# The MLP's first products: one four-byte pass becomes three rounded passes, and the gates move into the products' place

## The reference, cut to what matters

```python
DIM = 128
DEPTH = 2
HID = int(DIM * 4 * 2 / 3)
...
    x = x + o @ wo
    h = shift_token(x)
    mu = h.mean(-1, keepdims=True)
    var = h.var(-1, keepdims=True)
    h = (h - mu) / jnp.sqrt(var + 1e-05) * lg + lb
    h = h @ w1 + b1
    a, g = jnp.split(h, 2, axis=-1)
    h = a * jax.nn.gelu(g, approximate=False)
    x = x + h @ w2 + b2
```

## Time and profile before

| | |
|---|---|
| device time, median of 3 runs | 1245.42 us (1241.07 to 1248.66) |
| profiled execution | 1247.89 us |
| its span in the profile | 1246.1 us |
| busy: PE, DVE, ACT, POOL | 998.1, 798.1, 703.9, 390.8 us |
| mean granted PE clock | 0.922 of full speed |

### The profile page before, as it was taken

One profiled execution on the slowest core, in us unless ns is written; L12 is line 12 of the kernel. 1 busy time (PEld: TensorE's weight loads), 2 busy tenths in 40 slices (PEclk: granted clock), 3 DMA queues, 4 the chain that ended last, 5 costly groups with the idle time before them and its releaser, 6 DMA issues.

```text
span 1246.1 us, 22091 instructions
## 1 busy us (share of the span) xinstructions
PE 998.1 (80%) x8250; PEld 602.5 (48%) x8272; DVE 798.1 (64%) x1381; ACT 703.9 (56%) x1500; POOL 390.8 (31%) x251
## 2 busy tenths in 40 slices
PE   4079986069985788889889898989898898898886
PEld 2023333013323666666556665656565665666652
DVE  4088825058825668678677685867677786676751
ACT  3037763017773567557566565656666576576662
POOL 5000015000003553534444434342434435344330
PEclk9589998569997799999899999999999999999998
DMA  2950001950002211011010010000001010101100
GB/s 65 129 100 9 1 1 38 113 70 2 1 2 51 57 23 22 19 22 23 18 24 14 18 23 18 14 18 14 18 14 23 19 23 19 23 14 35 31 10 17
DMA packets 38268, 36.01 MB, mean 29 GB/s; under 512 B 11478, under 2 KB 30224, under 8 KB 38160
## 3 DMA queue, kind: packets, MB, share of 16 engines
q1 hardware_dynamic: 34708, 31.46, 13.8%
q10 hardware_dynamic: 3456, 3.15, 1.2%
HBM read 15.41 MB, written 4.21 MB: 16 GB/s over the span
## 4 chain that ended last, share of the span: by engine, by line
PE 28%; DVE 13%; POOL 11%; ACT 9%; issue 6%; POOLq 0%; DVEq 0%; ACTq 0%
PE psum L1165 6%; PE psum L1138 5%; POOL f_A L976 4%; POOL f_A L971 4%; ACT f_PW L1272 4%; PE psum L1052 3%; PE psum L1078 2%; PE psum L1089 2%; DVE f_A L1391 2%; DVE f_BS L1395 2%; POOL f_HL L963 2%; DVE f_NM L1423 2%; DVE f_SS L1402 2%; PE psum L1100 2%; PE psum L1158 1%
## 5 line engine op out<-in xcount | busy, mean ns | idle before, releaser
L1272 ACT ACTIVATE f_PW<-psum,f_NM 128x128 f32<-128x128 f32 x512 | 139.3, 383 | 127.9 <-DVE f_NM L1423 127.9
L500 DVE TENSOR_REDUCE a_M<-psum 128x1 f32<-128x512 f32 x256 | 160.2, 684 | 67.5 <-remote 38.7
L976 POOL TENSOR_TENSOR f_A<-f_A,f_RN 128x1024 f32<-128x1024 f32 x64 | 121.7, 1902 | 252.3 <-ACT f_RN L1283 250.0
L971 POOL TENSOR_TENSOR f_A<-f_A,f_BS 128x1024 f32<-128x1024 f32 x64 | 151.6, 2368 | 46.5 <-DVE f_BS L1395 45.0
L430 PE MATMUL psum<-a_KS,a_QS 128*128 128x512 bf16 x238 | 96.7, 413 | 79.7 <-DMA a_KS<-minus_ones 75.9
L547 ACT ACTIVATE a_PT<-psum 128x1024 f32<-128x1024 f32 x128 | 126.4, 1018 | 56.5 <-PE psum L452 56.1
L1391 DVE TENSOR_TENSOR f_A<-psum,cos 128x512 f32<-128x512 f32 x128 | 87.9, 686 | 93.5 <-ACT f_SQ L1240 93.5
L1052 PE MATMUL psum<-const,f_A 128*128 128x128 f32 x512 | 76.8, 299 | 49.6 <-POOL f_A L976 49.6
L452 PE MATMUL psum<-a_QS,a_KS 128*128 128x512 bf16 x252 | 94.5, 390 | 14.6 <-DMA a_QS<-a_MROW 10.4
L1423 DVE TENSOR_REDUCE f_NM<-psum 128x4 f32<-128x512 f32 x128 | 82.3, 685 | 36.4 <-PE psum L1078 36.4
L1042 PE MATMUL psum<-f_wqkv_h,f_HH 128*128 128x512 f32 x192 | 86.7, 451 | 23.0 <-DVE Y L1460 13.1
(11 more groups left out here) (173 smaller groups left out, 1966.5 us busy)
## 6 DMA issues: line engine op xcount, KB each, us to landing
f_VS<-f_V SPq DMA_DIRECT2D x112, 130.0 KB, 2.3
parts<-a_PRT ACTq DMA_DIRECT2D x24, 128.0 KB, 2.4
a_QS<-parts SPq DMA_DIRECT2D x8, 256.0 KB
a_KS<-parts SPq DMA_DIRECT2D x8, 256.0 KB
a_QS<-parts SPq DMA_DIRECT2D x4, 384.0 KB
a_KS<-parts SPq DMA_DIRECT2D x4, 384.0 KB
raw<-L_ffn_wqkv_dram SPq DMA_DIRECT2D x2, 768.0 KB, 7.0
a_XT<-L_attn_a_x_dram SPq DMA_DIRECT2D x4, 256.0 KB, 4.0
```

The costliest lines, as they stand in the source:

```text
L500: nc.vector.tensor_reduce(M[:, u % 4, k // 4, k % 4:k % 4 + 1], psum[:, bank("tile", i), :], AX_X, ALU.max)\
L971: nc.gpsimd.tensor_tensor(A[:, k % 2, :, :], A[:, k % 2, :, :], BS[:, k % 2, :, :], ALU.add)\
L976: nc.gpsimd.tensor_tensor(x, x, RN[:, k % 2, :, None].to_broadcast([P, 2 * HW, DW]), ALU.mult)\
L1272: last = nc.scalar.activation(PW[:, u % 4, c, :], psum[:, bank("scores", u), P * c:P * c + P], ACT.Exp, bias=NM[:, u % 4, c:c + 1])
```

## The change

The weights `w1` get a high part `w1_h` and a low part `w1_l`, for both layers at once (1364 columns). They are made at the start of `stream`: ACT waits for all weights and copies `w1_h` before it begins the plan, and POOL subtracts `w1_l` after its first three clears. For each group DVE rounds `mid` into `MH`, right after the bias, and POOL finds `ML = mid - MH` in the norm step. PE makes 18 products in `F32R` in place of the six plain ones, and waits for `mid_low` in place of `ln_done`. The buffer `gates` is gone: ACT writes the gates into `hidden`, once `w2` of the group before has read it, and DVE multiplies there in place. The raw `w1` lies in `hidden` until it is split, and `OUT` lies in `QB` and `NEG`.

```diff
-        w1 = sb("w1", [P, LAYERS, 2 * HID])
+        w1_h = sb("w1_h", [P, LAYERS, 2 * HID], F32R)
+        w1_l = sb("w1_l", [P, LAYERS, 2 * HID], F32R)
...
+        MH = sb("MH", [P, T], F32R)
+        ML = sb("ML", [P, T], F32R)
...
-        gates = sb("gates", [P, 3, T])
         hidden = sb("hidden", [P, 3, T])
+        w1 = hidden[:, :, :].rearrange("p b t -> p (b t)")[:, 0:LAYERS * 2 * HID]\
+            .rearrange("p (l n) -> p l n", l=LAYERS)
...
                 nc.gpsimd.memset(V[:, :, :, DW:DW + 1], 1.0).then_inc(s("zeroed"), 1)
+                pool.wait_ge(s("w1_high"), 1)
+                nc.gpsimd.tensor_tensor(w1_l[:, :, :], w1[:, :, :], w1_h[:, :, :].bitcast(F32), ALU.subtract)\
+                    .then_inc(s("w1_low"), 1)
                 nc.gpsimd.memset(VB[:, :, P:P + HA], 1.0).then_inc(s("ones_b"), 1)
...
                         pool.wait_ge(s("y_mid"), i + 1)
                         if i:
-                            pool.wait_ge(s("up"), 3 * i)
+                            pool.wait_ge(s("mid_low"), i)
...
+                    elif stage == "var" and norms[i][0] == "mlp":
+                        j = norms[i][1]
+                        pool.wait_ge(s("mid_high"), j + 1)
+                        if j:
+                            pool.wait_ge(s("up"), 3 * j)
+                        nc.gpsimd.tensor_tensor(ML[:, :], mid[:, :], MH[:, :].bitcast(F32), ALU.subtract)\
+                            .then_inc(s("mid_low"), 1)
...
-                        pe.wait_ge(s("ln_done"), i + 1)
+                        pe.wait_ge(s("mid_low"), i + 1)
                         for blk, (lo, w) in enumerate(HID_BLOCKS):
                             for kind, first in (("gate", HID), ("up", 0)):
-                                nc.tensor.matmul(take(kind, 3 * i + blk)[0:w, :],
-                                                 w1[:, layer, first + lo:first + lo + w],
-                                                 mid[:, :], start=True, stop=True).then_inc(s(kind), 1)
+                                dst = take(kind, 3 * i + blk)[0:w, :]
+                                of = slice(first + lo, first + lo + w)
+                                nc.tensor.matmul(dst, w1_h[:, layer, of], MH[:, :], start=True, stop=False)
+                                nc.tensor.matmul(dst, w1_l[:, layer, of], MH[:, :], start=False, stop=False)
+                                nc.tensor.matmul(dst, w1_h[:, layer, of], ML[:, :], start=False, stop=True)\
+                                  .then_inc(s(kind), 1)
...
                     nc.scalar.activation(wqkv_h[:, 0, cols], g.raw[:, cols], ACT.Copy).then_inc(s("weights_high"), 1)
+                act.wait_ge(s("weights"), 16 * len(weights))
+                nc.scalar.activation(w1_h[:, :, :], w1[:, :, :], ACT.Copy).then_inc(s("w1_high"), 1)
                 for stage, i in plan:
...
                             if i:
-                                act.wait_ge(s("hidden"), 3 * i + blk - 2)
-                            nc.scalar.activation(gates[0:w, blk, :], psum[0:w, bank("gate", 3 * i + blk), :],
+                                act.wait_ge(s("w2"), i)
+                            else:
+                                act.wait_ge(s("w1_low"), 1)
+                            nc.scalar.activation(hidden[0:w, blk, :], psum[0:w, bank("gate", 3 * i + blk), :],
                                                  ACT.Gelu, bias=b1[0:w, layer, 3 + blk:4 + blk])\
...
                             nc.vector.tensor_scalar(mid[:, :], mid[:, :], vecs[:, layer, 1:2], None, ALU.add)\
                               .then_inc(s("ln_done"), 1)
+                            dve.wait_ge(s("ln_done"), j + 1)
+                            if j:
+                                dve.wait_ge(s("up"), 3 * j)
+                            nc.vector.tensor_copy(MH[:, :], mid[:, :]).then_inc(s("mid_high"), 1)
```

More of the change, by code:

```diff
@@ L886, in stream @@
         OF = sb("OF", [P, T])
-        OUT = sb("OUT", [P, 2, 4, P])
+        OUT = [x[:, :].rearrange("p (t d) -> p t d", t=4) for x in (QB, NEG)]
         def pieces():
@@ L936, in _ @@
                         dst = out[k:k + 1].rearrange("a (t p) d -> p (a t) d", p=P)
-                        sp.dma_start(dst, OUT[:, k % 2, :, :]).then_inc(s(f"stored{k % 2}"), 16)
+                        sp.dma_start(dst, OUT[k % 2]).then_inc(s(f"stored{k % 2}"), 16)
                 for slot in range(4):
@@ L1360, in _ @@
                             act.wait_ge(s(f"stored{i % 2}"), 16 * (i // 2))
-                        nc.scalar.activation(OUT[:, i % 2, :, :].rearrange("p t d -> p (t d)"),
+                        nc.scalar.activation((QB, NEG)[i % 2][:, :],
                                              psum[:, bank("store", i), :], ACT.Copy).then_inc(s("out_copied"), 1)
@@ L1465, in _ @@
                             dve.wait_ge(s("gated"), 3 * i + blk + 1)
-                            if i:
-                                dve.wait_ge(s("w2"), i)
                             nc.vector.scalar_tensor_tensor(
                                 out=hidden[0:w, blk, :], in0=psum[0:w, bank("up", 3 * i + blk), :],
-                                scalar=b1[0:w, layer, blk:blk + 1], in1=gates[0:w, blk, :],
+                                scalar=b1[0:w, layer, blk:blk + 1], in1=hidden[0:w, blk, :],
                                 op0=ALU.add, op1=ALU.mult).then_inc(s("hidden"), 1)
```

## The result

The changed kernel takes 1257.61 us (median of 6 runs, 1254.85 to 1263.17) beside 1246.95 us of the kernel before (median of 6, 1235.48 to 1249.16). The ratio measured is 1.011, with a 95% interval of 1.0062 to 1.0159 (the two medians alone give 1.0085, inside it): slower, by about 1% and clear of the noise. The profiled execution took 1255.01 us, its span is 1253.2 us.

A forecast was written before the change was run, and what follows sets the result against it. It took DVE's maxima and ACT's line to bound each w1 step, PE adding 0.25 us in ten of 16 groups. Start +9.8, groups +2.1 and +1.8, last two -0.7 and -0.3 gave +12.7 us: 1258 us (1250 to 1266).

The forecast's parts named there:

- Start of `stream`: Head of the last part: ACT's copy waits for the last weight DMA, POOL's subtraction follows; first rotation sum +9.8 us.
- The second rival: The start costs little because later idle stretches take up most of the delay: about 1250 us, chance 9%.
- The cast: Norm step: DVE's rounding of mid between bias and maxima delays the maxima and ACT's line by 0.46 us a group.
- L1406 would be short: Norm step: this DVE maximum falls from 1.31 to 0.17 us without POOL's sum beside it, but gains nothing.
- The gates: w1 step: ACT's three gates shorten from 2.08 to 1.83 us in ten groups, -0.25 us each, since products end sooner.
- PE's gain of 1.0 us a group: w1 step: 18 rounded products take 4.3 us instead of 5.32; PE's busy time falls by some 15 us.
- ML and what it pushes: Norm and w1 steps: POOL's 1.28 us subtraction delays rotation sum and scaling, with 1.3 us to spare, costing nothing.
- the moved sum: Norm step: POOL's rotation sum could block DVE's cast or bias if already begun, but now stands behind both.
- The last groups: Groups 14 and 15, partly at half clock: faster products give -0.7 us and, after cast and subtraction, -0.3 us.
- The first rival: PE is the bound after all: fourteen groups gain 1.0 us each, the last two about 3 together; 1238 us, 5%.
- The third rival: PE, idle 1 us longer in each w1 step, falls to half clock more often: 1270 us, chance 7%.

The follow-up runs named there:

- run 1: Changed kernel with the two w1 transfers issued first and ACT waiting for these alone: 1249.19 us, ratio 1.0044 to the kernel before.
- run 2: As run 1, with the cast of mid into MH moved from DVE to POOL: 1243.2 us, ratio 0.9983 to the kernel before.
- run 3: Changed kernel with six plain four-byte products of the high parts, low-part products left out: 1261.3 us, ratio 1.0135 to the kernel before.
- run 4: Changed kernel with six rounded products of the high parts, low-part products left out: 1255.4 us, ratio 1.0088 to the kernel before.
- run 5: As run 2, with six plain four-byte products of the high parts, low parts left out: 1246.51 us, ratio 1.0008 to the kernel before.
- run 8: As run 7, plus cast, subtraction and PE's wait for them, but the old plain products of mid: 1256.43 us, ratio 1.0073 to the kernel before.
- run 6: As run 2, with DVE's bias after the maxima and POOL's cast and subtraction between rotation sum and scaling: 1238.81 us, ratio 0.9953 to the kernel before.
- run 7: Kernel before with only the gates' place changed, written into hidden and multiplied there in place: 1246.51 us, ratio 1.0013 to the kernel before.
- run 9: As run 6, with six plain four-byte products of the high parts, low parts left out: 1253.78 us, ratio 1.0039 to the kernel before.
- run 10: Kernel before with only the bias of mid moved behind the maxima on DVE: 1245.26 us, ratio 0.9998 to the kernel before.

## Why the prediction was right, and where its reasons were not

Predicted were 1258 us (1250 to 1266) and slower with 85%; measured were 1257.61 us and slower. The difference was to be +12.7 us; the median moved by 10.7, and the ratio's interval spans 7.7 to 19.8 us. In the profiled execution the terms of the sum come to 12.8 us (9.9, 3.6 and -0.8); the 3.5 us of half clock beside them are in no term.

- **Start of `stream`, +9.8 us: right, +9.93** (first square +9.14 for 9.1). The DMA landed 2.08 us after its issue began, 1.95 in the working. Run 1 shows that it is the wait and not the work. The second rival, idle time that takes the delay up, is ruled out for this kernel: run 1, which removes the delay, is 8.2 us faster by the ratios.
- **The cast, +0.46 us in 14 groups: right in ten (+0.47), too high in four (+0.34).** The working had noticed that L1406 would be short (0.17 us, as the earlier trace rows have 1.31) and put it at nothing, "since `mid` waits for ACT's `LR`". That holds in the ten. In the four, before and then changed:

```profile
719.96 0.73 DVE L1448 SCALAR_TENSOR_TENSOR f_mid<-psum,f_vecs,f_LR 128x512 f32<-128x512 f32 x1
```

```profile
720.18 0.75 DVE L1473 SCALAR_TENSOR_TENSOR f_mid<-psum,f_vecs,f_LR 128x512 f32<-128x512 f32 x1 [0.92 <-ACT f_LR L1343]
```

Before, DVE goes to `mid` without idle time there, so a shorter L1406 does help, until `LR` binds: counted from the squares of the norm step, `mid` starts at 6.03 us instead of 6.16. Every kernel in which L1406 is short in the norm step (the changed one, runs 1 to 5 and 8) has these 0.12 us, and those with 1.31 us (6, 7, 9 and 10) don't.

- **The gates, 2.08 to 1.83 us, -0.25 in ten groups: right in size, wrong in its cause.** The prediction said that PE gains 1.0 us, "So the gates turn from 2.08 to 1.83 us". Runs 3 and 8 have the same -0.25 with plain products. The cast makes ACT 0.46 us late, PE's line is not behind the cast and stays, and a wait of 0.25 us for PE vanishes by itself. The sum was right by luck: both causes remove the same 0.25 us, once.
- **PE's gain of 1.0 us a group: 0.9 in nine groups, less in five.** The 18 products last 4.43 us for 4.3 worked out, 4.67 in the four groups. All together they take 75.7 us of PE's time after 89.7, 14.0 less for the "some 15 us" of the working. The page shows only 7 us less, since PE's other rows are 7 us longer. Of that 1.7 us are ahead of `stream`, where the page of before lacks 22 records of products (L430 x238 and L452 x252, changed x256 each); in `stream` PE stood at half clock for 84 us after 73, counted from the first square.
- **ML and what it pushes, nothing: right.** 1.29 us, the scaling done 1.6 us before PE asks for it (1.3 in the working). That the moved sum could block cast or bias, had it begun, no run shows: it stands behind both.
- **The last groups, -0.7 and -0.3 us: -0.8 together by the end's time.** Against the last tile's squares the last gate of group 14 ends 0.8 us earlier (0.7 in the working). In group 15 PE starts its products 1.85 us after `mid` as worked out, and needs 6.9 us for 6.3, since the half clock lasted to 1243.1: from `mid` to the last product it is +0.3 us and not -0.3, inside the bounds given. As run 7's end is 1.7 us shorter with the old work, the agreement of the total is no proof.
- **The first rival, PE is the bound (5%), failed**: no group gained. Its mechanism needs DVE out of the way. Then the form is worth 0.78 us in ten groups (run 6 beside 9 or 10), near the 1.0 us that the rival put on it.
- **The third rival, more half clock (7%):** the changed kernel has 12 stretches for 10, and the other steps are 3.5 us longer. But run 7, with the same time as the kernel before, has 12 too (51 us), so this is not told apart from chance. The mechanism itself is real in run 4, where 4.4 us in five w1 steps go with it. By the Trainium skill, TensorE: Matmul & The Clock Gate, section "HAM oscillation", PE pauses between bursts cost clock again and again; run 4 agrees (72 us at half clock against 44), the changed kernel shows none of it in its w1 steps before the last two groups.

Open is why the part ahead of `stream` differs by up to 12 us between profiled executions of the same code (`stream` starts between 379 and 391 us). It is why the steps, not the spans, are compared here. Also open is why the stretches at half clock, and with them the pieces of 1.5 us, fall in other steps from one execution to the next.

## What to carry to other kernels

Before you make an engine faster, find by how much its successor actually waits for it: here 0.25 us of the 0.9 us saved. Then ask what the preparation of the faster form puts in front of whom: the cast on DVE cost 0.46 us a group and the faster products gave nothing there; with `w1` fetched first, the bias after the maxima and the cast on POOL the same change became 0.5% faster than the kernel before. And a wait for "all weights" at the head of an engine's program holds up everything behind it until the last one has landed (9.1 us of delay here for weights that ACT needed only in part); fetch first what is needed first, with a semaphore of its own.

A pair of experiments with and without the edit says what it is worth only for the order in which it was tried: the form was worth nothing per group in run 3, and in ten groups 0.26 us in run 5 and 0.78 us in run 9. Ask too whether the version without the edit still carries its cost, as run 9 does.

## What the runs showed of the hardware

- Fewer products don't always save their time: with six instead of 18 in a group, the mean granted clock was 0.904 to 0.911 in four executions, after 0.916 to 0.924 in six of the changed kernel, and five w1 steps with a stretch at half clock became longer by 4.4 us together.
- A 128 x 16 operation on DVE with two inputs in SBUF took 2.26 us at 402.43 in the changed kernel, where it ended with POOL's sum (402.32 + 2.34), and 0.17 us alone. Its delay carried on to ACT (`LN` began at 404.72, after 4.99 us of idle time that it ended). By the Trainium skill, SBUF — State Buffer, section "Who interferes with whom", this is the exclusive lock of a shared port, held for the whole instruction; the trace agrees.
- Rounding 128 x 512 from SBUF to SBUF took DVE 0.43 us and POOL 0.61 us, while the subtraction of the same size took POOL 1.29 us.
